# A two-layer graph kernel on one core: a reordered front, the logits' normaliser summed by a PE product, and GpSimd's bias additions one group later

## The reference, cut to what matters

```python
h = maximum(layernorm(x), 0)
node_att = softmax(h @ node_w, axis=0)              # over all 4096 nodes
g = h @ edge_w;  e = g @ g.T;  e = where(adj > 0, e, -9e15)
edge_att = softmax(e, axis=1)
x = x + (adj * (node_att * edge_att)) @ (h @ weight) + bias
h = maximum(layernorm(x), 0)
x = x + layer_1(h, adj, W1)                         # hyperbolic midpoint over the same neighbours
```

## Time and profile before

| | |
|---|---|
| time, three runs | 719.67, 722.23, 728.56 us (median 722.23) |
| the profiled execution | 725.74 us, of which the span is 724.0 |
| busy in the span | PE 495.6, DVE 471.4, POOL 396.6, ACT 350.2 us |
| mean granted clock of PE | 0.861 of full speed |
| a block of adjacency rows | 2048 KB, median 9.7 us from issue to landing |
| gathers of table_h | 160 of them, 1009 ns each |

### The profile page before, as it was taken

The page is one execution under the profiler, slowest core; times in us unless marked ns, Lnnn a source line. Parts: engine busy times, 40 slices in busy tenths (PEclk is TensorE's granted clock), DMA queues, the critical chain, the costliest instruction groups (busy, mean ns, idle before and its releaser), DMA issues.

```text
span 724.0 us, 12785 instructions
## 1 busy us (share of the span) xinstructions
PE 495.6 (68%) x3804; PEld 413.5 (57%) x3804; DVE 471.4 (65%) x1977; ACT 350.2 (48%) x718; POOL 396.6 (55%) x458
## 2 busy tenths in 40 slices
PE   3588463949698596988867877895266674757660
PEld 2367342738587485977766766784155553545440
DVE  3476757886877578686878578685444254476744
ACT  3596663655573555647340556477121121244553
POOL 4043537375655663566566610066477777777740
PEclk9798865959989899898989999998599798998885
DMA  8954579887879657786532400004433333335621
GB/s 310 394 204 173 189 283 366 291 314 254 291 232 369 219 219 266 244 342 211 185 94 67 101 17 1 1 1 148 147 97 99 103 100 97 97 106 159 193 75 59
DMA packets 38161, 128.92 MB, mean 178 GB/s; under 512 B 6224, under 2 KB 23504, under 8 KB 34000
## 3 DMA queue, kind: packets, MB, share of 16 engines
q1 hardware_dynamic: 22736, 84.87, 31.2%
q0 software_dynamic: 15360, 43.29, 21.3%
HBM read 115.49 MB, written 12.65 MB: 177 GB/s over the span
## 4 chain that ended last, share of the span: by engine, by line
PE 25%; DVE 25%; issue 13%; POOL 12%; ACT 9%; DMA 8%; DVEq 6%; ACTq 1%; POOLq 0%; SPq 0%
POOL work L1497 12%; PE bank L826 8%; DMA work<-in_adj 5%; PE bank L765 3%; ACT work L622 3%; DVE fs L1060 3%; PE bank L1589 2%; DVEq L1215 2%; PE bank L253 2%; PE bank L1768 2%; PE bank L797 2%; DMA table_h<-front 2%; DVE work L1104 1%; ACT L1211 1%; PE bank L810 1%
## 5 line engine op out<-in xcount | busy, mean ns | idle before, releaser
L720 POOL DMA_INDIRECT work<-table_h,work x160 | 161.4, 1009 | 99.6 <-issue 71.6
L1497 POOL DMA_INDIRECT work<-table_y,idx x128 | 130.7, 1021 | 39.0 <-issue 38.7
L622 ACT ACTIVATE work<-work 128x2048 bf16<-128x2048 f32 x64 | 121.6, 1902 | 45.6 <-DMA work<-in_adj 30.2
L826 PE MATMUL bank<-work 128*128 128x128 f32 x640 | 98.9, 318 | 15.7 <-DVEq L1106 15.7
L826 PEld LDWEIGHTS bank<-work 128*128 128x128 f32 x640 | 92.5, 230 | 17.5 <-DVEq L1106 15.0
L1589 PE MATMUL bank<-work 128*128 128x257 f32 x256 | 74.5, 442 | 19.8 <-DMA work<-table_y,idx 19.8
L765 PE MATMUL bank<-work 128*128 128x256 bf16 x512 | 70.8, 292 | 12.8 <-ACT work L622 12.8
L1589 PEld LDWEIGHTS bank<-work 128*128 128x128 f32 x256 | 55.4, 222 | 35.6 <-DMA work<-table_y,idx 26.4
L1585 PE MATMUL bank<-work 128*128 128x257 f32 x128 | 40.1, 440 | 48.9 <-ACT work L1600 40.5
L1362 DVE SCALAR_TENSOR_TENSOR fs<-work 128x256 f32<-128x256 f32 x32 | 13.7, 427 | 84.6 <-ACTq L1617 84.2
L765 PEld LDWEIGHTS bank<-work 128*128 128x128 bf16 x512 | 51.8, 104 | 27.3 <-ACT work L622 17.2
(11 more groups left out here) (271 smaller groups left out, 1006.6 us busy)
## 6 DMA issues: line engine op xcount, KB each, us to landing
work<-in_adj SPq DMA_DIRECT2D x32, 2048.0 KB, 9.7
table_y<-work SPq DMA_DIRECT2D x8, 520.0 KB, 3.7
gx<-in_x SPq DMA_DIRECT2D x8, 512.0 KB, 8.5
table_h<-front SPq DMA_DIRECT2D x8, 512.0 KB, 4.7
front<-in_x POOLq DMA_DIRECT2D x8, 512.0 KB, 5.0
out<-gx SPq DMA_DIRECT2D x8, 512.0 KB, 3.4
work<-table_h,work POOLq DMA_INDIRECT x160, 6.1
work<-table_y,idx POOLq DMA_INDIRECT x128, 2.8
```

What stands on the lines that cost most here:

```text
L622: a.activation(abf[:, u % HALVES, :], adu[:, b % 2, h, :], ACT.Copy, accum_out=cnt[:, k, b, h:h + 1]).then_inc(L["conv"], 1)
L720: p.indirect_dma_start(gat[:, k, n, :], None, table_h, bass.IndirectOffsetOnAxis(ix[:, k, n:n + 1], 0)) \
L826: last = t.matmul(bank[4 + b % 2][:, c * P:(c + 1) * P], gat[:, k, n, c * P:(c + 1) * P], otp[:, n, :], start=(q == 0), stop=(q == TILES - 1))
L1497: p.indirect_dma_start(gtm[:, n % OCT, q, :], None, table_y, bass.IndirectOffsetOnAxis(idx[:, n * TILES + q:n * TILES + q + 1], 0)) \
```

## The change

Seven edits:

1. SP's order of transfers in the front: the store of group 0 goes ahead of the load of block 1, of the last two loads of x and of the weights; x's group 5 is loaded ahead of it. Blocks 2, 3, 4, 5 are loaded behind the stores of groups 1, 2, 4, 6 (before: 1, 3, 5, 7).
2. ACT converts units 2 and 3 both in step 3, and units 4 to 7 in steps 4 to 7 (before: unit u in step u+1). Of group 1 it converts unit 0 in step 9 and unit 1 in step 10 (before: both in step 10).
3. PE packs units 2, 3 in step 4, units 4, 5 in step 6, unit 6 in step 7 and unit 7 in step 8 (before: unit u in step u+2).
4. DVE runs `keys` in steps 5 and 8 (before 6 and 9) and group 0's `edge_list` in step 9, ahead of step 10's body (before: behind it).
5. In step 1 of the sparse loop DVE runs `edges` before it waits for the maximum, and ACT converts units 2 to 7 of group 1 before it waits for the negated maximum.
6. The sum of the exponentials over partitions is a PE product of a 128 x 128 matrix of ones with the column of sums, in step 2, instead of POOL's second `partition_all_reduce`; DVE scales `natt` behind step 2's `dots`.
7. POOL adds the bias to group g's x behind group g+1's gathers and load of x, with a semaphore for each buffer.

The diff, with less context:

```diff
@@ -348,2 +348,3 @@
         s_exp = sem("s_exp")
+        s_sum = sem("s_sum")
 
@@ -524,2 +525,3 @@
         otp, o = arena(o, GT, P)
+        ones, o = arena(o, P)
         assert o <= WORK, o
@@ -548,2 +550,3 @@
         flag = sb("flag", [P, 1], I32)
+        exp_sum = bank[2][:, CH - 1:CH]
         t6b = bank[6][:, :].bitcast(BF16)
@@ -559,3 +562,2 @@
             "idx",
-            "x",
             "xb",
@@ -581,2 +583,3 @@
         L["adj"] = [sem(f"fa_adj{n}") for n in range(2)]
+        L["x"] = [sem(f"fa_xr{k}") for k in range(2)]
         L["gat"] = [[sem(f"fa_gat{k}{b}") for b in range(GB)] for k in range(2)]
@@ -592,2 +595,3 @@
             p.memset(upper, 1.0)
+            p.memset(ones, 1.0)
             p.memset(bad[:, :], 0.0)
@@ -611,2 +615,5 @@
         EARLY = GB + 2
+        STORED = (1, 2, 4, 6)
+        CONV_AT = (1, 2, 3, 3, 4, 5, 6, 7)
+        PACK_AT = (2, 3, 4, 4, 6, 6, 7, 8)
 
@@ -626,7 +633,7 @@
             def beside(n):
-                if 1 <= n <= UNITS * GB:
-                    unit_conv(a, 0, 0, n - 1)
-                if n == NG + 2:
-                    unit_conv(a, 1, 1, 0)
-                    unit_conv(a, 1, 1, 1)
+                for u in range(UNITS * GB):
+                    if n == CONV_AT[u]:
+                        unit_conv(a, 0, 0, u)
+                if n > NG:
+                    unit_conv(a, 1, 1, n - NG - 1)
             return beside
@@ -664,7 +671,2 @@
 
-                if ls and not at_:
-
-                    a.wait_ge(s_negmax, 1)
-                    a.activation(natt[:, :], logit[:, :], ACT.Exp, bias=cs(1)[:, 1:2], accum_out=cs(0)[:, 2:3])
-                    a.drain().then_inc(s_exp, 1)
                 n = ag_[0] + 3 if ag_ and isinstance(ag_[0], int) else 0
@@ -687,2 +689,6 @@
                     conv(u, wd)
+                if ls and not at_:
+                    a.wait_ge(s_negmax, 1)
+                    a.activation(natt[:, :], logit[:, :], ACT.Exp, bias=cs(1)[:, 1:2], accum_out=cs(0)[:, 2:3])
+                    a.drain().then_inc(s_exp, 1)
                 for b in (2, 3):
@@ -723,4 +729,6 @@
                     p.wait_ge(L["x1"], GB * g + GB)
-                    p.dma_start(xr2[:, k, :, :], x_r[:, grp(g), :]).then_inc(L["x"], 16)
-                    p.wait_ge(L["x"], 16 * (g + 1))
+                    p.dma_start(xr2[:, k, :, :], x_r[:, grp(g), :]).then_inc(L["x"][k], 16)
+                if at_:
+                    g, k = at_
+                    p.wait_ge(L["x"][k], 8 * (g - k) + 16)
                     for b in range(GB):
@@ -773,4 +781,5 @@
             def beside(n):
-                if 2 <= n <= UNITS * GB + 1:
-                    unit_pack(t, 0, n - 2, (6, 7))
+                for u in range(UNITS * GB):
+                    if n == PACK_AT[u]:
+                        unit_pack(t, 0, u, (6, 7))
             return beside
@@ -880,2 +889,5 @@
                 exp_g(0, GT // 4)
+                if at_ and not ag_:
+                    t.wait_ge(s_exp, 1)
+                    t.matmul(exp_sum, ones, cs(0)[:, 2:3], start=True, stop=True).then_inc(s_sum, 1)
                 pack(2)
@@ -938,6 +950,8 @@
             def beside(n):
-                if n == 6:
+                if n == 5:
                     keys(d, 0, 0, 0, (6, 7))
-                if n == NG + 1:
+                if n == NG:
                     keys(d, 0, 0, 1, (6, 7))
+                if n == NG + 1:
+                    edge_list(d, 0, 0, None)
                 if n == NG + 2:
@@ -946,3 +960,2 @@
                     d.drain().then_inc(s_red, 1)
-                    edge_list(d, 0, 0, None)
             return beside
@@ -1116,7 +1129,2 @@
                 if ls and not at_:
-
-                    d.wait_ge(s_all, 1)
-                    d.tensor_scalar(cs(1)[:, 1:2], cs(1)[:, 0:1], -1.0, None, ALU.mult)
-                    d.drain().then_inc(s_negmax, 1)
-                if ls and not at_:
                     for k in (0, 1):
@@ -1125,7 +1133,6 @@
                     edges(*ls)
-                if at_ and not ag_:
-                    d.wait_ge(s_all, 2)
-                    d.reciprocal(cs(1)[:, 3:4], cs(1)[:, 2:3])
-                    d.drain()
-                    d.tensor_scalar(natt[:, :], natt[:, :], cs(1)[:, 3:4], None, ALU.mult)
+                if ls and not at_:
+                    d.wait_ge(s_all, 1)
+                    d.tensor_scalar(cs(1)[:, 1:2], cs(1)[:, 0:1], -1.0, None, ALU.mult)
+                    d.drain().then_inc(s_negmax, 1)
                 n = ag_[0] + 3 if ag_ and isinstance(ag_[0], int) else 0
@@ -1150,2 +1157,8 @@
                     dots(*at_, GT // 4, GT // 2)
+                if at_ and not ag_:
+                    d.wait_ge(s_sum, 1)
+                    d.reciprocal(cs(1)[:, 3:4], exp_sum)
+                    d.drain()
+                    d.tensor_scalar(natt[:, :], natt[:, :], cs(1)[:, 3:4], None, ALU.mult)
+                if at_:
                     by_slot(*at_)
@@ -1862,8 +1875,3 @@
             load(4)
-            e.dma_start(w0[:, :, :], weight.rearrange("(c p) d -> p c d", p=P)).then_inc(s_w2, 16)
-            e.dma_start(w1[:, :, :], W1.rearrange("(c p) d -> p c d", p=P)).then_inc(s_w2, 16)
-            e.dma_start(bias_bc[:, :], bias.rearrange("(a d) -> a d", a=1).broadcast_to([P, D])).then_inc(s_w2, 16)
-            for g in range(5, NG):
-                load(g)
-            load_block(e, 1, 1)
+            load(5)
 
@@ -1872,6 +1880,14 @@
                 e.dma_start(th_r[:, grp(g), :], hs[:, k, :, :]).then_inc(s_th[k], 16)
-            for g in range(NG):
+            store(0, 0)
+            load_block(e, 1, 1)
+            load(6)
+            load(7)
+            e.dma_start(w0[:, :, :], weight.rearrange("(c p) d -> p c d", p=P)).then_inc(s_w2, 16)
+            e.dma_start(w1[:, :, :], W1.rearrange("(c p) d -> p c d", p=P)).then_inc(s_w2, 16)
+            e.dma_start(bias_bc[:, :], bias.rearrange("(a d) -> a d", a=1).broadcast_to([P, D])).then_inc(s_w2, 16)
+            for g in range(1, NG):
                 store(g, g % 2)
-                if g % 2:
-                    load_block(e, g // 2 + 2, g // 2 % 2)
+                if g in STORED:
+                    n = STORED.index(g) + 2
+                    load_block(e, n, n % 2)
             fast_load(e)
@@ -1921,5 +1937,2 @@
             p.drain().then_inc(s_all, 1)
-            p.wait_ge(s_exp, 1)
-            p.partition_all_reduce(cs(1)[:, 2:3], cs(0)[:, 2:3], P, RADD)
-            p.drain().then_inc(s_all, 1)
             p.wait_ge(s_w2, 48)
```

8 lines of the change are left out of this document (4 added, 4 removed).

## The result

The changed kernel takes 734.1 us (median of 5 runs, 732.62 to 741.67), where the kernel before took 722.23 (median of 5, 719.67 to 728.56): a ratio of 1.0162, with a 95% interval of 1.0116 to 1.0209. The forecast was 716.4 us with a range of 709 to 722.5, so the sign is wrong and the time lies outside the range. The execution that the profiler saw took 741.67 us (span 740.0), 7.5 us above its median, while the one of before lay 3.5 above; so the losses read from its rows are larger than those of the medians. It was also the slowest of the five.

What follows compares the result with a forecast made beforehand. Work the change leaves alone leads the chain, so gains lie in single stalls, mostly of the front. Edits 1 to 5 -8.2, ones product +0.3, later bias +2.1: -5.8 from 722.2 gives 716.4 us, range 709 to 722.5.

Steps and rivals of the forecast that it cites:

- part 5: POOL's bias additions one group later: no loss in steps 4 to 8, `new_x` late in step 9, +2.1 us.
- Parts 1 and 2: Front: group 0's store loses its 7.8 us stall, net -3.5 us; `keys` and packing gain 2.7 and 0.5; running sum -6.7.
- Part 3: Front's end, `keys` and `edge_list` ahead of step 10's body: group 1's `edge_list` at 105.4 instead of 113.6 us, -8.2 in all.
- The contention rival: Loop steps 3 to 7: earlier gathers lengthen block loads by 1.25 us each, +12 us, 728 us; chance 0.1.
- The ports' rival: Loop steps 4 and 6 to 8: POOL's additions hold DVE 0.8 us a step, +3.2, 719.6 us; chance 0.08.
- The stall only moves: Front: stream full until 38 us, ACT waits for blocks 1, 2 and the second store instead; 721.6 us, chance 0.12.
- Part 4: Sum of exponentials as PE's ones product in step 2: POOL's sum was hidden, the product costs +0.3 us.

Runs made afterwards that it cites:

- e1: The changed kernel with POOL's bias additions back in their old place behind the same group's gathers, drain kept: 725.19 us, ratio 1.0014.
- e3: The changed kernel with POOL's bias additions at the head of its next step, ahead of the next group's gathers: 722.76 us, ratio 0.9978.
- e17: The kernel of e1 once more, in a later job: 725.85 us, ratio 1.003.
- e7: The changed kernel without the drain behind the four bias additions, each addition signalling by itself: 726.03 us, ratio 1.0037.
- e11: The kernel before, unchanged, entered once more against itself: 724.24 us, ratio 0.9963.
- e10: The changed kernel with bias additions back, no drain, group 1's units 0 to 3 converted in step 9, maximum negated behind group 1's first `keys`: 717.89 us, ratio 0.9914.
- e16: The kernel of e10 once more, in a second job: 720.2 us, ratio 0.9979.
- e2: The kernel before with only the bias additions moved one group later: 741.27 us, ratio 1.0227.
- e12: The kernel before with only the sum of exponentials moved from POOL to a PE product with ones: 723.71 us, ratio 0.9986.
- e8: The kernel before with only the new order of conversions, packing, `keys`, `edge_list`, `edges` and exponentials: 740.78 us, ratio 1.0266.

## Why the prediction was wrong

Two terms add up to the miss: -5.8 us forecast, 734.1 - 722.2 = +11.9 measured. The six other edits: -5.8 - 2.1 = -7.9 us forecast, +0.5 measured (the mean ratio of e1, e3 and e17, 1.0007, which can't be told from nothing). Edit 7: +2.1 forecast, +11.2 measured by the ratios. So 716.4 + 8.4 + 9.1 = 733.9, against 734.1.

**The step that gave the wrong sign is part 5**, "In steps 4 to 8 it comes 2 us behind their end (211.82 against 209.7), so nothing", and "In step 9 ... the additions end at 417.0 ...: +2.1 us". Both take the end of the additions for the moment at which `new_x` is released. The signal is sent by the drain, 1.8 to 3.8 us later. The row that showed it was on the page of rows: the gather at 216.89 us with 2.79 us of "issue" ahead of it. The prediction used that very number, as the lead of the next gather, and didn't ask what POOL did in it. With 2.3 us more the margin of 2 us is gone, and `new_x` waited for L736 in steps 3, 6, 7, 8 and 9; e7, which takes only the drain away, brings back 8 of the 9.5 us. In step 9 the wait is 10.28 us instead of 6.01, 4.3 us more: near the 2.1 that were forecast and the 2.3 of the drain. Two smaller things were missed. The first additions of all stand behind 11.64 us of "issue", at whose start their line has the instruction that the first reduction has:

```profile
L735 POOLq MODIFY_POOL_CONFIG  x2: 58/58/58, 151.1 to 151.1; - x2
```

POOL's timeline of the kernel before has such a stall too, with the same instruction at 127.7 us:

```profile
135.66 2.77 POOL L727 TENSOR_TENSOR front<-front,bias_bc 128x256 f32<-128x256 f32 x4 [8.03 <-issue]
```

It lay there in a step in which nobody waited for it; edit 7 moves it right ahead of `new_x` of group 0, which costs 3.33 us in the changed kernel and nothing in e7, where the drain doesn't come on top. And PE, having stood 4.9 us, pays 2.5 us more for its next products.

**The order's gain was right in the front and wrong in the sum.** Parts 1 and 2 hold: 23.57 us for the normalisation (23.2 forecast), waits of 0.52 and 0.94 us (0.6 and 1.5), `edges` at 83.60 (83.6). Part 3 looks 2.8 us too good in the profile of the changed kernel (block 7's conversion at 98.14 us, the maximum's wait 4.25), but holds in the six others with the same instructions up to there: the conversion at 95.8 to 97.5 us (96.8 forecast), the wait 2.4 to 2.9 (2), `edge_list` of group 1 at 104.4 to 106.3 (105.4). The stall ahead of POOL's reduction, 9.1 to 11.0 us and not 6.6, was missed; it costs nothing there, as DVE still waits for PE's last units behind it. But then the sum carries this gain to the end of the kernel one to one, on "the loop repeats in 41 us, with no stall that these edits remove", and this failed: e17 has `edge_list` of group 1 at 104.4 us, 9.2 earlier than before, and group 7's mark at 437.36 us, where before has 437.3. In these two profiles ACT waits longer for blocks. The same group of lines in the window from 113 to 280 us and in that from 280 to 440 us, before:

```profile
L622 ACT ACTIVATE work<-work 128x2048 bf16<-128x2048 f32 x32 | 60.7, 1901 | 24.9 <-DMA work<-in_adj 20.7 <-issue 4.2
...
L622 ACT ACTIVATE work<-work 128x2048 bf16<-128x2048 f32 x16 | 30.4, 1901 | 10.1 <-DMA work<-in_adj 5.3 <-PE bank L765 4.2 <-issue 0.6
```

and in e17:

```profile
L629 ACT ACTIVATE work<-work 128x2048 bf16<-128x2048 f32 x30 | 56.9, 1900 | 28.5 <-DMA work<-in_adj 27.8 <-issue 0.7
...
L629 ACT ACTIVATE work<-work 128x2048 bf16<-128x2048 f32 x16 | 30.4, 1900 | 10.6 <-DMA work<-in_adj 10.0 <-issue 0.6
```

That is 26.0 us of waits for blocks before and 37.8 in e17. Four blocks of 9.7 us against a step of 41 us leave the loop little room if one follows the other, and a chain that arrives earlier would wait for its blocks. Against this reading stand some numbers: the same windows give 31.1 us for the kernel before in e11, 31.6 in e3, and 34.0 and 32.5 in e10 and e16, which keep a part of their gain. Another 1.7 us of the 6.3 that e17 loses in the loop lie in the step with the loop's turn, which the old front shows too (e2, e12). The marks of the loop differ as much between two kernels with the same order of instructions (432.0 in e3, 437.4 in e17). So the loss is shown, and its cause isn't: block loads are the likeliest, no run made them lighter, and the cause stays open. The step that failed is the one that took the loop to hand the gain on whole. Nor is all of a gain in the front lost: e10 and e16 arrive 11 us early and keep 2 to 6.

**The rivals.** The contention rival gave 728 us and the right sign by another mechanism. A block lands in 9.7 us in the median in the changed kernel as before, and ACT's waits for blocks in the two windows above are 33.8 us with the additions late, no more than with them back (31.6 and 37.8 in e3 and e17), so gathers that start earlier didn't stretch the block loads. Only e8 shows a contention, and there it is the load of x that suffers beside the blocks (15.39 us). The ports' rival is real and small. In the changed kernel L1056 of DVE takes 0.82 us beside the additions; in e3, where they are elsewhere, it takes 0.48 (over steps 3 to 8 it is 0.57 to 1.00 us in five of six, and always 0.48 in e3):

```profile
209.68 0.82 DVE L1056 TENSOR_TENSOR work<-work 128x320 f32<-128x320 f32 x1
```

```profile
201.85 0.48 DVE L1056 TENSOR_TENSOR work<-work 128x320 f32<-128x320 f32 x1
```

The Trainium skill, "SBUF — State Buffer", section "SBUF: two separate sides", calls the pair of ports that the two engines share an exclusive lock, so that DVE's instruction would wait for the addition in flight; the row agrees, at 0.34 us. "The stall only moves", 721.6 us with a chance of 0.12, came closest to what the six other edits did, though by another way: the front's stream gave the gain that was forecast, and the loop lost it.

**Part 4 held** for the product by itself: it is worth nothing. What was missed is that it is the condition for edit 5, which would cost 3.5 to 5 us without it.

## What to carry to other kernels

A wait is released by the instruction that signals, not by the one that computes: where a drain stands between, take its time from the "issue" gap behind the work, and compare the consumer with the end of that gap. Before a gain in a prologue is carried to the end of the kernel, look for the loop's second limit (here perhaps loads of 2 MB, four of 9.7 us to a step of 41 us): of 5 to 9 us gained in the front, none was left in the median. A single profile can be off by as much as the effect that is read from it: the front of the changed kernel looked 2.8 us short in one and was as forecast in six. Where an edit moves work to a later turn of an engine's queue, its one-off stalls move too, and one that nobody waited for can land on the path.
